# Convolution, attention and mixture-of-experts block on one core: the score shift as a product row, merged query-key weights, and biases carried by a constant channel

## The reference, cut to what matters

```python
# layer 0, on channels x positions, per image
theta, phi = theta_w @ xf, phi_w @ xf            # 64 channels each
f = softmax(theta.T @ phi / sqrt(64))            # 1024 x 1024
x = x + proj_w @ (f applied to xf)
t = tokens(x)                                    # 1024 tokens x 128 channels
# layer 1, attention on normalised tokens z = ln(t)
keys, queries, values = z @ Wk + bk, z @ Wq + bq, z @ Wv + bv
t = t + softmax(queries @ keys.T / sqrt(128)) @ values
# experts on z = ln(t): 8 experts, the two best of each token
top_w, top_i = top_k(z @ Wg + bg, 2)
t = t + sum over the two of softmax(top_w) * (gelu(z @ W1[e] + b1[e]) @ W2[e] + b2[e])
```

## Time and profile before

| what | us |
|---|---|
| median of 3 timed runs (560.21 to 565.96) | 565.32 |
| span of the profiled execution, first to last instruction | 603.2 |
| PE busy in it | 431.2 |
| DVE busy | 431.8 |
| ACT busy | 300.6 |
| POOL busy | 307.6 |

### The profile page before, as it was taken

The page is one execution under the profiler, slowest core; times in us unless marked ns, Lnnn a source line. Parts: engine busy times, 40 slices in busy tenths (PEclk is TensorE's granted clock), DMA queues, the critical chain, the costliest instruction groups (busy, mean ns, idle before and its releaser), DMA issues.

```text
span 603.2 us, 15423 instructions
## 1 busy us (share of the span) xinstructions
PE 431.2 (71%) x4139; PEld 313.6 (52%) x4140; DVE 431.8 (72%) x1303; ACT 300.6 (50%) x689; POOL 307.6 (51%) x352
## 2 busy tenths in 40 slices
PE   5668898999999899995952051610588898989626
PEld 3333565766666567663741041400476687878512
DVE  4897898988889788888684131781277788878737
ACT  4567766668866556663541000130265566656402
POOL 2012264555466654553787737027047677767720
PEclk9899999999999899998885565855699999999965
DMA  6100400000000130000011101004312222222166
GB/s 205 29 2 0 140 1 0 3 0 3 0 1 0 30 112 0 1 0 2 10 53 54 53 28 53 1 22 114 78 40 74 71 74 83 74 76 84 45 198 238
DMA packets 33493, 30.94 MB, mean 51 GB/s; under 512 B 8327, under 2 KB 27437, under 8 KB 33453
## 3 DMA queue, kind: packets, MB, share of 16 engines
q1 hardware_dynamic: 28844, 20.92, 12.2%
q0 software_dynamic: 4608, 9.51, 4.7%
HBM read 16.69 MB, written 13.73 MB: 50 GB/s over the span
## 4 chain that ended last, share of the span: by engine, by line
PE 25%; DVE 22%; issue 21%; POOL 8%; another core or an unknown queue 8%; ACT 7%; DVEq 3%; SPq 2%; DMA 2%; ACTq 1%; POOLq 0%
PE SC L529 8%; PE PV L529 7%; PE MX L529 6%; POOL ybuf L517 5%; PE PR L529 3%; DVE mx L1179 3%; ACT E L987 2%; DVE DG L1183 2%; ACT EH L911 1%; DVE TOK L1475 1%; DVE stats L1218 1%; DVE TOK L1480 1%; DVE QK L1137 1%; DVE TOK L1214 1%
## 5 line engine op out<-in xcount | busy, mean ns | idle before, releaser
L529 PE MATMUL PV<-VH,EH 128*128 128x129 f16 x512 | 98.2, 230 | 9.2 <-DVE TOK L1214 7.5
L529 PE MATMUL PV<-VL,EH 128*128 128x128 f16 x512 | 97.8, 226 | 3.6 <-issue 3.6
L529 PE MATMUL PV<-VH,EL 128*128 128x129 f16 x512 | 98.1, 228 | 2.2 <-issue 2.2
L474 POOL TENSOR_TENSOR EL<-E,EH 128x1024 f32 (+1 forms) x32 | 68.1, 2128 | 59.6 <-ACT EH L911 59.3
L517 POOL DMA_INDIRECT ybuf<-QK,yid x80 | 88.4, 1105 | 18.2 <-issue 12.8
L910 ACT ACTIVATE E<-SC 128x512 f32<-128x512 f32 x128 | 77.1, 602 | 37.5 <-PE SC L529 37.5
L529 PE MATMUL SC<-QK 128*128 128x512 f16 x320 | 91.0, 383 | 6.3 <-ACT EH L911 5.9
L438 POOL DMA_INDIRECT zbuf<-ZZ,posi x64 | 63.5, 993 | 51.9 <-DVE posi L1104 33.6
L1179 DVE TENSOR_REDUCE mx<-MX 128x1 f32<-128x1024 f32 x64 | 77.9, 1217 | 1.5 <-PE MX L529 1.1
L911 ACT ACTIVATE EH<-SC 128x512 f32 (+1 forms) x128 | 77.8, 608 | 0.0
L529 PE MATMUL MX<-EL,EH 128*128 x640 | 59.4, 246 | 2.7 <-issue 2.7
(11 more groups left out here) (195 smaller groups left out, 963.5 us busy)
## 6 DMA issues: line engine op xcount, KB each, us to landing
EH<-zbuf SPq DMA_DIRECT2D x40, 130.0 KB
X<-in_x_dram SPq DMA_DIRECT2D x4, 512.0 KB, 5.6
zbuf<-zer SPq DMA_DIRECT2D x16, 128.0 KB, 2.8
X<-in_L_ffn_W_dram SPq DMA_DIRECT2D x1, 2048.0 KB, 9.7
EL<-ybuf SPq DMA_DIRECT2D x4, 512.0 KB, 5.6
EH<-ybuf SPq DMA_DIRECT2D x4, 512.0 KB, 8.9
out_dram<-X SPq DMA_DIRECT2D x8, 256.0 KB, 3.0
ybuf<-QK,yid POOLq DMA_INDIRECT x80
```

Source lines behind the costliest of these rows:

```text
L474: nc.gpsimd.tensor_tensor(EL[:, u % 2, ds(i * 2 + 1, 1), :], E32[:, 1:2, :], EH[:, u % 2, ds(i * 2 + 1, 1), :], ALU.subtract).then_inc(e32 ...
L529: return nc.tensor.matmul(o, w, r, start=start, stop=stop)
```

## The change

- **Maxima.** No `DG`. The row maxima are written as two bfloat16 columns `mxb`. A new function `row` on PE multiplies them with a negative scaled identity, which gives one row of 256 numbers in partition 0 of `MX`; ACT copies it into partition 0 of the queries' low half `QL`. In layer 0 the keys' new second tile `KL` has a constant in partition 0 (partitions 1 to 63 are zero, 64 to 127 hold the keys' high half), in layer 1 the keys' partition 0 is the constant channel. So the product with `QL` subtracts the maximum. Scores take two products in layer 0 (three before) and three in layer 1 (four before).
- **Order.** `SC` has one bank per key tile of the pair now; the first half of the queries is done for both key tiles, then the second. `EL` is split between DVE and POOL by half of the queries.
- **Constant channel.** Channel 0 of z is the constant 128. Row 0 of each weight is the bias over 128, and the old row 0 is subtracted from all other rows (`augment`, for attention and router, `expert_rows` for W1), since channel 0 is minus the sum of the others. The bias products, the bias adds and gelu's bias operand are gone; gelu is one instruction of 1024 columns per tile.
- **Merged weights.** Query and key weights are multiplied once; the normalised tokens themselves are the keys of layer 1. Its keys' projection, copy and low half are gone.
- **Set-up.** POOL fills the constants of `QK` and `ZZ` before PE's first work; SP loads broadcast rows of the weights, for W1 eight of 256 KB.

Cut to its core, the diff is:

```diff
+CST = 128.0
+TOP = 2.0 ** 15
...
-        DG = sb("DG", [P, 2, T, P], BF16)
-        mx = sb("mx", [P, T], F32)
+        mxb = sb("mxb", [P, 2], BF16)
         ident16 = sb("ident16", [P, P], F16)
-        identb = sb("identb", [P, P], BF16)
+        negI = sb("negI", [P, 2, P], BF16)
...
-                {"rows": (0, 0), "values": (1, 0), "queries": (0, 1), "keys": (1, 1)},
+                {"rows": (0, 0), "values": (1, 0), "queries": (0, 1)},
...
-            for j, w in enumerate((Wq, Wk, Wv)):
-                sp.dma_start(W32[:, 2 + j, :], w).then_inc(b_in, 16)
-            sp.wait_ge(bias_zeroed, 1)
-            for j, v in enumerate((bq, bk, bv)):
-                for r in (0, 32):
-                    sp.dma_start(B32[r:r + 1, j, :], v).then_inc(b_in, 16)
-            sp.dma_start(Wg32[:], Wg).then_inc(g_in, 16)
-            sp.dma_start(bgb[:], bg.partition_broadcast(P)).then_inc(g_in, 16)
-            sp.dma_start(b1r[:], b1).then_inc(g_in, 16)
+            for j, (w, bias) in enumerate(((Wq, bq), (Wk, bk), (Wv, bv))):
+                sp.dma_start(W32[1:P, 2 + j, :], w[1:P, :]).then_inc(b_in, 16)
+                sp.dma_start(W32[0:1, 2 + j, :], bias).then_inc(b_in, 16)
+                sp.dma_start(W0b[:, j, :], w[0, :].partition_broadcast(P)).then_inc(b_in, 16)
+            sp.dma_start(Wg32[1:P, :], Wg[1:P, :]).then_inc(g_in, 16)
+            sp.dma_start(Wg32[0:1, :], bg).then_inc(g_in, 16)
+            sp.dma_start(Wg0b[:], Wg[0, :].partition_broadcast(P)).then_inc(g_in, 16)
...
-            sp.wait_ge(mx_full, mx_base(1) + 1)
-            sp.dma_start(Xw.rearrange("p (e h) -> p e h", e=E), W1.rearrange("e d h -> d e h")).then_inc(wexp_in, 16)
+            sp.wait_ge(mx_full, mx_base(1) + 2)
+            sp.dma_start(Xw[1:P].rearrange("p (e h) -> p e h", e=E), W1.rearrange("e d h -> d e h")[1:P]) \
+                .then_inc(w1_in, 16)
+            sp.dma_start(Xw[0:1], b1).then_inc(w1_in, 16)
+            for e in range(E):
+                sp.dma_start(W10b[e // PAIRS][:, e % PAIRS * HID:(e % PAIRS + 1) * HID],
+                             W1[e, 0, :].partition_broadcast(P)).then_inc(w1_in, 16)
...
-            nc.gpsimd.tensor_copy(identb[:], ident32[:]).then_inc(const_ready, 1)
+            for j, c in enumerate((TOP, CST)):
+                nc.gpsimd.tensor_scalar(negI[:, j, :], ident32[:], -1.0 / c, None, ALU.mult).then_inc(const_ready, 1)
+            nc.gpsimd.memset(QK[0:CE, :, 1, :], 0.0).then_inc(preset, 1)
+            nc.gpsimd.memset(QK[0:CE, :, 3, :], 0.0).then_inc(preset, 1)
+            pool.wait_ge(preset, 2)
+            nc.gpsimd.memset(QK[0:1, :, 3, :], TOP).then_inc(preset, 1)
+            nc.gpsimd.memset(ZZ[:, :, 0:1], CST).then_inc(preset, 1)
+            nc.gpsimd.memset(ZZ[:, :, P:P + 1], 0.0).then_inc(preset, 1)
...
             pe.wait_ge(const_ready, 4)
+            pe.wait_ge(preset, 5)
...
+                def row(unit, need):
+                    pe.wait_ge(mx_free, need)
+                    for p in range(2):
+                        last = mm(MX[0:1, p * P:(p + 1) * P], mxb[:, p:p + 1], negI[:, layer(unit), :], True, True)
+                    last.then_inc(mx_full, 1)
...
+                        pe.wait_ge(augmented, 1)
+                        nc.tensor.transpose(GR[:, 0:P], W32[:, 2, :], ident32[:])
+                        nc.tensor.transpose(GR[:, P:2 * P], W32[:, 3, :], ident32[:]).then_inc(aug_full, 1)
...
+                    kl = KL[:, w, ds(i * 256 + p * P, P)]
+                    pe.wait_ge(sc_free, i * 4 + (2 * T * u + 2 * h + p + 1))
                     c = slice(h * HALF, (h + 1) * HALF)
-                    o_ = SC[:, h, :]
+                    o_ = SC[:, p, :]
                     mm(o_, kh, QH[:, w, c], True, False)
-                    mm(o_, kh, QL[:, w, c], False, False)
                     if u >= B:
-                        mm(o_, KL[:, w, ds(i * 256 + p * P, P)], QH[:, w, c], False, False)
-                    pe.wait_ge(diag_ready, T * u + T // 2 * (h + 1))
-                    mm(o_, onesb[:], DG[:, u % 2, 4 * h:4 * h + 4, :], False, True).then_inc(sc_full, 1)
+                        mm(o_, kh, QL[:, w, c], False, False)
+                        last = mm(o_, kl, QH[:, w, c], False, True)
+                    else:
+                        last = mm(o_, kl, QL[:, w, c], False, True)
+                    last.then_inc(sc_full, 1)
...
-                        scores(i, 0, 1)
+                        scores(i, 1, 0)
+                    if first and u is not None:
+                        row(u, mx_base(s) + 1)
+                    if not first and m is not None:
+                        row(m, i * 3 + n_mx)
                     if first and v is not None and v < B:
                         residual_stream()
                     if first and a is not None:
                         for p in range(2):
                             pe.wait_ge(e32_free[p], PAIRS * (a + 1) + 1)
+                        pe.wait_ge(pr_free[2], uses_before(a + 3, 2) + 1)
                     if a is not None:
                         outputs(i, 0)
                     if u is not None:
-                        scores(i, 1, 0)
+                        if first:
+                            pe.wait_ge(mx_free, mx_base(s) + 2)
...
+                def row(unit, c, need):
+                    act.wait_ge(mx_full, need)
+                    cp(QL[0:1, unit % 3, c], MX[0:1, 0:2 * P]).then_inc(mx_free, 1)
...
-                    act.wait_ge(wexp_in, 16)
+                    act.wait_ge(w1_augmented, PAIRS)
...
-                for c in range(HC):
-                    k = slice(c * TR, (c + 1) * TR)
-                    last = nc.scalar.activation(h32[:, b % 2, k], WIDE[b % 2][:, k], ACT.Gelu,
-                                                bias=b1T[:, ds(e * HC + c, 1)], scale=1 / WS)
-                last.then_inc(h_ready, 1)
+                nc.scalar.activation(h32[:, b % 2, :], WIDE[b % 2], ACT.Gelu, scale=1 / WS).then_inc(h_ready, 1)
...
+            def augment():
+                dve.wait_ge(vecs, 2)
+                dve.wait_ge(b_in, 16 * 9)
+                nc.vector.scalar_tensor_tensor(out=W32[:, 2:5, :], in0=W0b[:], scalar=nvec[:, 0:1],
+                                               in1=W32[:, 2:5, :], op0=ALU.mult, op1=ALU.add)
+                dve.wait_ge(g_in, 48)
+                nc.vector.scalar_tensor_tensor(out=Wg32[:], in0=Wg0b[:], scalar=nvec[:, 0:1], in1=Wg32[:],
+                                               op0=ALU.mult, op1=ALU.add).then_inc(vecs, 1)
+                dve.wait_ge(vecs, 3)
+                nc.vector.tensor_scalar(Wg32[:], Wg32[:], svec[:, 0:1], None, ALU.mult)
+                nc.vector.tensor_scalar(W32[:, 2:5, :], W32[:, 2:5, :], svec[:, 0:1], None, ALU.mult) \
+                    .then_inc(augmented, 1)
...
+            def expert_rows(k):
+                c = slice(k * S, (k + 1) * S)
+                nc.vector.scalar_tensor_tensor(out=Xw[:, c], in0=W10b[k // 2][:, k % 2 * S:(k % 2 + 1) * S],
+                                               scalar=nvec[:, 0:1], in1=Xw[:, c], op0=ALU.mult, op1=ALU.add) \
+                    .then_inc(w1_augmented, 1)
...
+                if s == 3:
+                    dve.wait_ge(w1_in, 16 * (2 + E))
+                    for k in range(PAIRS):
+                        expert_rows(k)
...
-                    nc.vector.reduce_max(mx[:, p:p + 1], MX[:], AX.X).then_inc(mx_free, 1)
-                def diagonals(i, p):
-                    dve.wait_ge(mx_free, i * 2 + (n_mx + p + 2))
-                    nc.vector.tensor_scalar(DG[:, m % 2, ds(i * 2 + p, 1), :], identb[:], mx[:, p:p + 1], -1.0,
-                                            ALU.mult, ALU.mult).then_inc(diag_ready, 1)
+                    dve.wait_ge(mx_full, i * 3 + (n_mx + p + 1))
+                    nc.vector.reduce_max(mxb[:, p:p + 1], MX[:], AX.X).then_inc(mx_free, 1)
...
-                    elif on_a:
+                    if on_a and not (on_v and v < UNITS):
                         take_wait()
                     if on_a:
                         statistics(i, 0)
+                        sums(i, 1)
                         counted(i, 0)
-                    if on_m:
-                        diagonals(i, 0)
+                    if on_v and v < UNITS:
+                        queries(i)
                     elif on_a:
                         take_wait()
                     if on_a:
                         moments(i, 0)
```

241 lines of the change are left out of this document (127 added, 114 removed).

## The result

The changed kernel takes 604.12 us (median of 4 runs, 603.79 to 608.61), the kernel before beside it 562.77 (558.85 to 565.96). The ratio is 1.0754, with a 95% interval of 1.0688 to 1.082: 41 us slower, where 6.6 us faster was forecast. The profiled execution took 604.42, with a span of 602.6.

The account below looks back on a forecast made before the run. No engine was above 72%, so the kernel was taken as bound by different things in different stages. The terms summed to -6.6 us, taking 565.3 to 558.7; the 8-in-10 range was 545 to 572.

Parts of the forecast that it names:

- The loads for them have two steps' time: Before step 3: the broadcast loads that expert_rows needs were taken to have two steps' time to arrive.
- Start: Kernel start: POOL's three long memsets at 2.6 us each delay PE's beginning to near 10.5; +5.2 us.
- augmented weights: Before the first maxima: four DVE operations on the weights, then two transposes, with PE waiting; +1.5 us.
- Row trips in step -1: Step -1: the new row's product and ACT copy occupy MX, 0.8 us per pair, three times; +2.4 us.
- Step 0: Step 0: one product less per tile about equals what the key and row copies add to ACT; 0.
- rival B: Slower: row trip not hidden, PE waits for ACT's copy, steps 1 to 6 lose 12.8; 571.5 to 577, chance 0.16.
- Steps 1, 2, 5, 6: Loop pairs: less work on PE and DVE shortens each pair by 0.5 to 0.9; -2.0, -3.2, -3.6, -3.0 us.
- Step 3: Step 3: -4.0 without the keys' copy, against +6.1 for expert_rows at its head; +2.1 us.
- Step 4: Step 4: diagonal goes, its stall beside POOL's conversion passes to the mean's copy, pair 9.53 to 9.3; -1.0 us.
- term of the first pairs: Heads of steps: PE's waits for the last diagonals shrink, partly returning as waits for the row; -2.0 us.
- Expert tiles: Expert phase: one gelu instead of four saves 0.5 us in seven or eight tiles; -3.0 us.
- Step 7 and the scatters: From step 7 on: POOL's work stays the same; 0. Unexplained idle times belong to the profiled execution only.

Follow-up runs that it names:

- start_whole: Changed kernel with W1 and the start's weights loaded in 128 rows, presets late, row of the maxima in mid-block; 570.42 us, ratio 1.0117.
- no_row: Changed kernel with W1 loaded in 128 rows, presets late and the row of the maxima left out whole; 557.82 us, ratio 0.99.
- presets_late_2: Changed kernel with W1 loaded in 128 rows and POOL's presets moved to the end of its prologue; 581.43 us, ratio 1.0325.
- best: Changed kernel with all edits: whole-row loads, late presets, row mid-block, spread expert_rows, second bank first, ACT's wait moved; 559.11 us, ratio 0.9914.
- w1_whole_3: Changed kernel with W1 loaded in all 128 rows and b1 written over row 0 after landing; 582.83 us, ratio 1.035.
- before_sizes: Kernel before with ten more loads from W1 into a spare buffer, differing in number of rows and first row; undisturbed profile, 562.3 us.
- before_gelu1: Kernel before with one gelu instruction of 1024 columns per tile, b1 left out; 561.45 us, ratio 0.9953.
- before_split: Kernel before with W1 loaded as rows 1 to 127 and row 0 separately; 627.66 us on a disturbed chip, ratio 1.0432.

## Why the prediction was wrong

It named the loads in one sentence, "The loads for them have two steps' time", and that is **the step that failed**. They had it, if they were issued. I counted how long DVE may wait and not how long the transfer ahead in SP's queue runs. The changed load has one row less than the old one, and I took it for the old one. It cost 21.7 us by experiment, 45% of the 48 between the forecast of -6.6 and the measured +41.

The others, by the terms of the sum:

- *Start, +5.2, and augmented weights, +1.5*: +9.6 together. The memsets took 2.65 us each where I had 2.6; that is luck, since the row that I worked from (0.52 us for 512 columns) makes 3.1 of 3072. PE began at 11.22 where I had 10.5, and ACT's first copy of the image came at 12.51 instead of 6.80, +5.7. The other 3.9 lie between that copy and the first maximum: the augmentation is the mis-sized term. Its four DVE operations took 1.3 us; that PE stands 3.64 us for them, with the first maxima's products queued behind, I had not counted. Behind that wait the clock stood at 0.50, and these two products took 1.06 us where the kernel before has 0.59. With the presets and the loads mended 3.1 us of it stay (6.10 to 22.25 in start_whole, 6.80 to 19.82 before). Without the presets the 127-row loads hold the start, as start_whole showed.
- *Row trips in step -1, +2.4*: +6.0, of which no_row gives back 5.2. The trip is 0.93 us and not 0.8, a pair 1.1 longer, and there is a fourth row that I had left out. It lies between the last maxima of the step and the first of the next, with ACT's copy behind 1.9 us of other work (50.66 to 52.56); that stretch took 10.95 us (46.01 to 56.96, clock 0.69) where it was 8.34 (clock 1.00). My own sign, PE's wait before the row above a few tenths, stood at 1.51.
- *Step 0, 0*: +4.5. The row's absence takes presets_late_2's 33.99 to 27.08, below the 27.87 before. I had weighed ACT's work and not asked what the row does in a ring that nobody fills. This is rival B's mechanism in a place where I had not put it.
- *Steps 1, 2, 5, 6*, forecast -11.8: in the changed kernel steps 1 and 5 make -0.7, a pair of step 2 takes 8.36 against 8.30, and one of step 6 is 0.38 shorter where I had 0.75. The work did leave PE and DVE, the ring did not close: the row stood ahead of 24 products. In `best` steps 1, 2, 3 and 5 together are 7.2 us shorter than before, so the relief was there and the order of the work hid it.
- *Step 3, +2.1*, with `expert_rows` at +6.1: the +6.1 is right in mechanism and size, the rest of the term isn't. Once the loads are in time, steps 2 and 3 take 74.48 us (w1_whole_3) against 69.22, +5.3. That is 6.4 for `expert_rows` and -1.2 in step 3, where I had 7.2 of relief for the two steps together.
- *Step 4, -1.0*: -3.9. The stall passed to the copy of the mean, as forecast with the Trainium skill's rule; the timeline of DVE in step 4 of the changed kernel has it:

```profile
238.35 1.98 DVE L1307 COPY mean<-mv 128x2 f32<-128x2 f32 x1
247.34 2.07 DVE L1307 COPY mean<-mv 128x2 f32<-128x2 f32 x1
```

  A pair takes 9.07 (forecast 9.3, before 9.53). The greater part, 2.8 us, came in the last stretch of the step, from 11.64 to 8.87. Half of it isn't the change's: the kernel before has 11.64 and 11.63 there at a clock of 0.85 (before, before_sizes) but 10.20 and 10.19 at 1.00 (before_gelu1, before_split). The other 1.3 fit the diagonals: PE stood 2.21 us there for the last of them, which belongs to the term of the first pairs.
- *Expert tiles, -3.0*: -2.5 by before_gelu1. The size is right, but its derivation leaned on tiles of 3.35 us that only a disturbed execution has.
- *Step 7 and the scatters, 0, and the idle times*: right. Without them the span and the run agree within 2 us, and POOL's scatters are the bound from step 7 to the tiles. The group of the page for them in the changed kernel:

```profile
L464 POOL DMA_INDIRECT zbuf<-ZZ,posi x64 | 64.1, 1002 | 18.9 <-issue 18.9
```

Of the rivals, B named the row and 12.8 us for it; the row cost about 24, half of them in steps that B left out. (Its 12.8 also leave out the 4.0 that I had for step 3.) None had a load that becomes slower by being one row shorter. The range's upper end, 572, would have held the changed kernel only with the loads, the presets and the row's place mended: start_whole, which has all three, took 570.4.

## What to carry to other kernels

A transfer is part of the change as soon as its shape is: count the engines that it gets and follow its queue to the last issue behind it, above all when a slice loses a row. Load whole and overwrite. And a new link in a ring (here the row) is priced in the ring that is emptiest, not in the one that is fullest; where a queue has independent work, put that work ahead of the link's wait, and look at what stands ahead of the link in the other engine's list.

## What was new about the hardware

- A load of 127 rows of 2 KB took 12.85 us, one of 126 took 2.69. The 2032 KB of `W1` in 127 rows ran at 26 to 28 GB/s for some 75 us; 2048 KB in 128 rows landed within 9.6.
- The queue that issued it stood still at the next issue, 74.69 us (74.60 in the other kernel). At the start of the changed kernel SP stood 2.81 to 5.15 us at each bias load, a load into one partition, behind 127 rows; in the kernel before two such loads behind 128 rows were issued in 0.60. A transfer that nobody waits for yet can so delay all that its queue issues later. Every issue that stood was of a load into one partition; whether one on all engines would have stood too is open.
- A memset on POOL took 2.65 us for 3072 columns in 64 partitions and the same in one partition.
- In the sessions on two of the chips each of these kernels stood idle for tens of us behind step 7 without a releaser that the profile knows: 8% of the chain in before_split, none in the changed kernel, whose chips were others. What it is stays open.
